# First experts of a decoder kernel: the residual add in four tiles, and a root of nine operations

## The reference

```
x = x + attention0(ln(x));  x = x + cross0(ln(x), ctx)
x = x + experts0(ln(x));    x = x + states(ln(x))
x = x + cross1(ln(x), ctx); x = x + experts1(ln(x))

ln(v)    = (v - mean) / sqrt(var + 1e-5)
experts0 = sum over 8 experts e of c[:, e] * ((silu(v W1 + B1) * (v W3 + B3)) W2 + B2)
           + a shared expert of the same form with weight 1
```

## Time and profile before

| | |
|---|---|
| median of 3 runs | 332.16 us |
| the profiled execution | 332.09 us |
| its span, first to last instruction | 330.4 us |
| mean granted TensorE clock | 0.906 |
| TensorE busy (matmul) | 267.2 us, 81% |
| VectorE busy | 216.7 us, 66% |
| ScalarE busy | 147.4 us, 45% |
| GpSimd busy | 63.6 us, 19% |
| chain that ended last | TensorE 40%, VectorE 13%, ScalarE 3% of the span |

### The profile page before, as it was taken

The page is one execution under the profiler, slowest core; times in us unless marked ns, Lnnn a source line. Parts: engine busy times, 40 slices in busy tenths (PEclk is TensorE's granted clock), DMA queues, the critical chain, the costliest instruction groups (busy, mean ns, idle before and its releaser), DMA issues.

```text
span 330.4 us, 5158 instructions
## 1 busy us (share of the span) xinstructions
PE 267.2 (81%) x1783; PEld 178.8 (54%) x1788; DVE 216.7 (66%) x775; ACT 147.4 (45%) x298; POOL 63.6 (19%) x71
## 2 busy tenths in 40 slices
PE   0898799995885889599499438863898989999994
PEld 0344677775542456456266224352387855666774
DVE  4638695697348546516823887799057768888974
ACT  2174654552440496344545402512445665444442
POOL 4346880000000034211423300112213000000000
PEclk9999799998796999879979756985699999999999
DMA  6368900029210000000000000000000000000002
GB/s 165 65 199 200 285 15 0 2 32 285 36 32 0 2 0 1 3 1 0 0 0 2 0 1 0 0 2 2 0 3 2 3 2 1 0 2 0 3 0 64
DMA packets 22038, 11.62 MB, mean 35 GB/s; under 512 B 11016, under 2 KB 21005, under 8 KB 22013
## 3 DMA queue, kind: packets, MB, share of 16 engines
q1 hardware_dynamic: 21117, 11.01, 13.0%
q0 software_dynamic: 80, 0.20, 0.6%
q10 hardware_dynamic: 816, 0.10, 0.2%
HBM read 8.68 MB, written 2.62 MB: 34 GB/s over the span
## 4 chain that ended last, share of the span: by engine, by line
PE 40%; DVE 13%; ACT 3%; issue 2%; DVEq 0%; ACTq 0%
PE bank L874 8%; PE bank L862 7%; PE bank L792 3%; PE bank L755 3%; PE bank L732 3%; PE bank L738 2%; PE bank L847 2%; PE bank L811 2%; DVE XN L1372 2%; PE bank L526 1%; DVE stats L1330 1%; PE bank L774 1%; PE bank L834 1%; DVE Es L1600 1%; DVE sm L1597 1%
## 5 line engine op out<-in xcount | busy, mean ns | idle before, releaser
L498 POOL TENSOR_TENSOR X<-X,att 128x512 f32<-128x512 f32 x18 | 22.8, 1269 | 116.2 <-ACT att L1182 116.2
L1546 DVE SCALAR_TENSOR_TENSOR att<-bank,cols,att 128x512 f32<-128x512 f32 x18 | 13.5, 751 | 27.1 <-ACT att L1171 14.6
L874 PE MATMUL bank<-Wb,att 128*128 128x128 f32 x256 | 30.8, 277 | 0.0
L874 PEld LDWEIGHTS bank<-Wb,att 128*128 128x128 f32 x256 | 29.7, 192 | 1.4 <-issue 1.4
L862 PE MATMUL bank<-XT,Wb 128*128 128x512 f32 x64 | 30.0, 599 | 0.0
L526 PE MATMUL bank<-ident,XN 128*128 128x128 f32 x48 | 10.0, 344 | 24.0 <-DVE XN L1372 24.0
L1182 ACT ACTIVATE att<-bank,comb 128x128 f32<-128x128 f32 x72 | 20.5, 370 | 18.2 <-PE bank L755 11.6
L755 PEld LDWEIGHTS bank<-W2a,att 128*128 128x128 f32 x144 | 20.3, 204 | 10.4 <-issue 5.2
L755 PE MATMUL bank<-W2a,att 128*128 128x128 f32 x144 | 22.3, 295 | 2.1 <-DVE att L1546 2.1
L1218 ACT ACTIVATE att<-bank 128x512 f32<-128x512 f32 x32 | 18.8, 598 | 9.1 <-PE bank L862 9.1
L526 PEld LDWEIGHTS bank<-ident,XN 128*128 128x128 f32 x48 | 6.9, 176 | 28.6 <-DVE XN L1372 25.8
(11 more groups left out here) (235 smaller groups left out, 544.7 us busy)
## 6 DMA issues: line engine op xcount, KB each, us to landing
Wb<-in_L_ffn_W SPq DMA_DIRECT2D x1, 1024.0 KB, 5.6
Wb<-in_L_ffn_W SPq DMA_DIRECT2D x8, 128.0 KB, 5.3
X<-in_x SPq DMA_DIRECT2D x2, 256.0 KB, 3.0
k_scratch<-QKVT SPq DMA_DIRECT2D x1, 512.0 KB, 2.6
q_scratch<-QKVT SPq DMA_DIRECT2D x1, 512.0 KB, 3.1
Wb<-k_scratch SPq DMA_DIRECT2D x1, 512.0 KB, 4.8
V<-q_scratch SPq DMA_DIRECT2D x1, 512.0 KB, 5.5
v_scratch<-QKVT SPq DMA_DIRECT2D x1, 512.0 KB, 6.1
```

Of the source, the lines that this page charges most:

```text
L498: nc.gpsimd.tensor_tensor(X[:, h * HT:(h + 1) * HT, :], X[:, h * HT:(h + 1) * HT, :], part0[:, i % 2, :, :], ALU.add).then_inc(f_acc, 1)
L874: last = mm(bank[4 + h][:, t * P:(t + 1) * P], hid[:, e % 2, f, tile], W2b[:, e, f, :], start=(f == 0), stop=(f == F1 - 1))
```

## The change

GpSimd adds tile by tile: four operations of 128 x 128 for each step, each of which waits for its own tile of `part0` and for the same tile's add of the step before. So ScalarE raises `f_part` after each tile, and the other waits for the two semaphores count tiles. The root's guess becomes one operation (the bits of var, read as an integer, times -0.5 plus the constant, written as an integer), and both steps are replaced by one polynomial of fourth degree in y = r*r*var: nine operations in the same three pieces, four, three and two. The tile `magic` and its semaphore go.

```diff
+    ROOT = (2.46301634, -3.28812578, 2.96127482, -1.41023935, 0.27407397)
...
-            nc.gpsimd.memset(magic[:, :], 0x5f3759df).then_inc(c_magic, 1)
...
-                    pool.wait_ge(f_part, i + 1)
-                    if i >= 1:
-                        pool.wait_ge(f_acc, i)
-                    nc.gpsimd.tensor_tensor(X[:, h * HT:(h + 1) * HT, :], X[:, h * HT:(h + 1) * HT, :],
-                                            part0[:, i % 2, :, :], ALU.add).then_inc(f_acc, 1)
+                    for t in range(HT):
+                        pool.wait_ge(f_part, HT * i + t + 1)
+                        if i >= 1:
+                            pool.wait_ge(f_acc, HT * (i - 1) + t + 1)
+                        nc.gpsimd.tensor_tensor(X[:, h * HT + t, :], X[:, h * HT + t, :], part0[:, i % 2, t, :],
+                                                ALU.add).then_inc(f_acc, 1)
...
-                    pe.wait_ge(f_part, i - 1)
+                    pe.wait_ge(f_part, HT * (i - 1))
...
-                    pe.wait_ge(f_part, 2 * (E0 + 1))
+                    pe.wait_ge(f_part, 2 * HT * (E0 + 1))
...
-                    act.wait_ge(f_acc, i - 1)
+                    act.wait_ge(f_acc, HT * (i - 1))
                 for t in range(HT):
                     tt = HT * h + t
-                    last = AF(part0[:, i % 2, t, :], bank[4 + i % 2][:, t * P:(t + 1) * P], ACT.Copy,
-                              scale=comb[:, tt, e:e + 1])
-                last.then_inc(f_part, 1)
+                    AF(part0[:, i % 2, t, :], bank[4 + i % 2][:, t * P:(t + 1) * P], ACT.Copy,
+                       scale=comb[:, tt, e:e + 1]).then_inc(f_part, 1)
...
             def root_guess(h):
-                r, var, bits = rs[:, 0, tiles(h)], rs[:, 1, tiles(h)], rs[:, 4, tiles(h)]
+                r, var, y, t = (rs[:, i, tiles(h)] for i in range(4))
                 then(V.tensor_scalar(var, mv[:, tiles(h), 1], EPS, None, ALU.add))
-                then(V.tensor_scalar(bits.bitcast(int32), var.bitcast(int32), 1, None, ALU.logical_shift_right))
-                then(V.tensor_tensor(r.bitcast(int32), magic[:, :], bits.bitcast(int32), ALU.subtract))
+                then(V.tensor_scalar(r.bitcast(int32), var.bitcast(int32), -0.5, float(0x5f3759df), ALU.mult, ALU.add))
+                then(V.tensor_tensor(t, r, r, ALU.mult))
+                then(V.tensor_tensor(y, t, var, ALU.mult))
 
             def root_third(h):
-                r, var, y2, p = (rs[:, i, tiles(h)] for i in range(4))
-                then(V.tensor_tensor(y2, r, r, ALU.mult))
-                then(V.tensor_tensor(y2, y2, var, ALU.mult))
-                then(V.tensor_scalar(p, y2, 0.375, -1.25, ALU.mult, ALU.add))
-                then(V.tensor_tensor(p, p, y2, ALU.mult))
-                then(V.scalar_tensor_tensor(r, p, 1.875, r, ALU.add, ALU.mult))
+                y, t = rs[:, 2, tiles(h)], rs[:, 3, tiles(h)]
+                then(V.tensor_scalar(t, y, ROOT[4], ROOT[3], ALU.mult, ALU.add))
+                then(V.tensor_tensor(t, t, y, ALU.mult))
+                then(V.scalar_tensor_tensor(t, t, ROOT[2], y, ALU.add, ALU.mult))
 
             def root_second(h):
-                r, var, y2, p = (rs[:, i, tiles(h)] for i in range(4))
-                then(V.tensor_tensor(y2, r, r, ALU.mult))
-                then(V.scalar_tensor_tensor(p, y2, -0.5, var, ALU.mult, ALU.mult))
-                then(V.scalar_tensor_tensor(r, p, 1.5, r, ALU.add, ALU.mult))
+                r, y, t = rs[:, 0, tiles(h)], rs[:, 2, tiles(h)], rs[:, 3, tiles(h)]
+                then(V.scalar_tensor_tensor(t, t, ROOT[1], y, ALU.add, ALU.mult))
+                then(V.scalar_tensor_tensor(r, t, ROOT[0], r, ALU.add, ALU.mult))
...
-                    dve.wait_ge(f_acc, (E0 + 1) * (h + 1))
+                    dve.wait_ge(f_acc, HT * (E0 + 1) * (h + 1))
```

More of the change, by code:

```diff
@@ L90, in decoder_kernel @@
         jconst = sb("jconst", [P, NC, E1], int32)
-        magic = sb("magic", [P, HT], int32)
         vecs = sb("vecs", [31, P])
@@ L209, in decoder_kernel @@
         c_ident = sem("c_ident")
-        c_magic = sem("c_magic")
         c_azero = sem("c_azero")
@@ L1398, in first_max @@
                 then(V.tensor_tensor(one_hot, em8[:, cut, :], per_row(rv[:, 4, cut], E0), ALU.is_equal))
-            dve.wait_ge(c_magic, 1)
             for h in range(2):
```

## The result

| | before | after |
|---|---|---|
| median of four runs each, same chip, us | 332.75 (332.11 to 333.63) | 320.80 (320.44 to 321.50) |
| ratio to before | 1 | 0.965 (0.962 to 0.968) |
| profiled execution, us | 332.09 | 321.50 |
| its span, us | 330.4 | 319.8 |
| its mean granted clock | 0.906 | 0.915 |

The change takes 12 us away, 3.5%. Forecast were 327.9 us and a range of 325.4 to 330.2: the sign was right and the size far too small. The profiled executions differ by 10.6 us, and these 10.6 us are what the traces can account for. Executions in the slower of the chip's two states are left out of every comparison; the only one is the first profiled execution of the kernel before kept busy (330.7 us, the other three 325.2 to 326.1).

A forecast was written before the change was run, and what follows sets the result against it. Neither TensorE nor VectorE alone was the bound: work changes hands where TensorE waits for VectorE's XN. From 332.09 us, 3.8 for roots and 0.4 for holds came off, giving 327.9 us, range 325.4 to 330.2.

The forecast's parts named there:

- The roots, 3.8 us: Layer norms' roots on VectorE: nine operations for eleven save 0.40 us each where TensorE waits; 3.8 us, bounds 2.2 to 4.2.
- The holds, 0.4 us booked: VectorE's root operations held by GpSimd's adds: 4.4 us instead of 5.1, 0.7 gained on paper, 0.4 booked.
- rival (c): TensorE's lower clock after idling, at 137 to 146 us or behind 165 and 194: 325.5 or 330.3; chance faster 0.12, slower 0.05.
- (a): GpSimd/VectorE port: VectorE can't get between tile adds, stalls grow by 1.8 us, 330.1 us; chance 0.15.
- (b): Roots of the run's first half are hidden: they save 2.2 us instead of 3.8, 329.5 us; chance 0.07.
- (d): ScalarE's writes, 116 to 186 us: signalling each breaks their overlap, 0.34 us a group, 334.0 us; chance 0.03.
- (e): GpSimd's add still waits for all four tiles, 328.3 us; chance 0.58 together with the forecast.
- The test named in advance: Mean granted clock off 0.906 by more than 0.01 would show that (c), not the roots, made the difference.

The follow-up runs named there:

- kernel before kept busy: Kernel before plus 10 and 12 unread bf16 matmuls (the fillers) ahead of the transposes at 137.01 and 164.99: 325.69 us, ratio 0.983; again 325.51 us, 0.982.
- The root alone: Kernel after with one add of 128x512 and one signal a group again, keeping the new nine-operation root: 327.17 us, ratio 0.988 to the kernel before.
- the second execution: Kernel after run once more, unchanged, with a second profile: 320.61 us, ratio 0.964 to the kernel before, span 318.7.
- the pauses: Kernel after with seven more 4-element products (1.4 us) behind the root at each of two places: 326.68 us, ratio 0.986 to the kernel before.
- the late version: Kernel after, but each of the four adds waits until all four tiles are written: 323.77 us, ratio 0.974 to the kernel before.

## Why the prediction was wrong in size

**The roots, 3.8 us: right.** The root alone gave 4.0 us, but 1.6 of its profiled gain were clock, so that this number agrees partly by luck; the waits show the term better. At undisturbed places XN is ready 0.39 us sooner, with nine operations 0.2 apart, and the int32 guess lasts 0.17 like its neighbours. One of the nine was lost in the profiled execution: the first transposes start 0.32 us sooner (8.18 for 8.50), and the first scores 0.2 later (29.46 for 29.27), with the next transposes taking 0.99 us in the kernel after for 0.60 in the one before. That is not the clock, which was granted 1.00 there in both, and in the second execution they take 0.60 and the scores start at 28.43. The waits that the roots shorten sum to some 3.5 us.

**The holds, 0.4 us booked: the first step that failed.** They fell from 5.1 to 2.5 us, a gain of 2.6. The prediction gave a held operation 0.36 us and let it delay the adds. In the trace a held operation lasts 0.38, so it waits 0.21, and the adds don't wait for VectorE: four take 1.69 whether it is between them or not. The start-to-start distance is (1.69 - 0.456)/3 = 0.41 us, so the 0.40 was right; what was wrong is the cycle around it. The next add has already begun while the released operation runs its 0.17, so from one release to the next it is 0.41 us in all, of which 0.17 are the operation and 0.03 lie between two of them; 0.21 are left as the hold. Against the change the Trainium skill (GPSIMD Engine Reference, Elementwise — side-by-side cycle accounting) had led to an estimate of 0.44 for a tile; measured are 0.456 for one alone and 0.41 in a row. It changed little: by the working above the hold hangs on the pace and not on the length.

**The gate's hold: left out.** The prediction does not mention it, and so put it at nothing without a reason. In the kernel before, an operation inside the gate of the second half was held. Timeline of VectorE, then of TensorE:

```profile
151.74 1.13 DVE L1395 TENSOR_TENSOR rt<-rt,rv 128x32 f32<-128x32 f32 x1
```

```profile
158.70 1.16 PE L755 MATMUL bank<-W2a,att 128*128 128x128 f32 x8 [0.83 <-DVE att L1546]
```

Against the ordinary 0.19 us it was held 0.94; in the kernel after two of the gate's operations last 0.41 and 0.34, held 0.37 together. ScalarE waits for the gate's result before it weighs an expert's output (4.00 us of idling, ended at 156.08 by L1537; 3.43 in the kernel after). Its silu, VectorE's product and TensorE's matmul follow in turn, and the wait at the last of them falls from 0.83 us to 0.26 (at 152.76). These 0.57 us belong to the same term: the holds gave 3.1 us in all where 0.4 stood.

**The clock, rival (c), 12%: the second step that failed.** It stood beside the forecast as an accident, at "about 2.4 us" for half of a stretch; half of the 3.4 us that it had worked out is 1.7, so the 2.4 has no working. TensorE's timeline gives its real size: from XN's transpose at 137.01 to the expert matmuls at 145.29 the kernel before loses 3.3 us to the kernel after (5.37 of shift less 2.04 already there), and behind 166 us another 1.6: 4.9 us on the path, both stretches whole. The fillers give the same 3.3 and 1.6 us with VectorE's work untouched, the pauses take them away again. The prediction had named the two places and the idling, and its 3.4 us for the first was nearly right; but it did not let the shorter waits of its own sum carry the clock with them. Roots and holds together took 1.3 and 1.1 us off these two waits, and behind both the level was low.

**Sum over the profiled executions.** Roots gave 3.5 and holds with the gate's 3.1; of the 10.6 us that leaves 4.0 for the clock and everything else. The two stretches gave 4.9, and 0.9 were lost elsewhere, some 0.4 ahead of 137 us and the rest behind 194 us. One such loss lies from 83 to 88 us, 1.2 us: the matmuls at L543 took 1.92 us for 1.51 and those at L546 1.91 for 1.02, at the low level. The second execution of the kernel after divides otherwise: of its 11.7 us the two stretches hold 3.3, and 1.8 come from elsewhere. So where the clock pays differs from execution to execution. Both leave 4 to 5 us beyond roots and holds, of which 4.9 and 3.3 are shown to be the clock's at the two places.

**The rivals.** (a), the port turned against the change: refuted, nothing is held longer than one tile's add. (b): only one of the four early roots was lost. (d): refuted, four writes with four signals take 1.14 us as with one. (e): the adds do begin when written; the late version costs 3 us. The test named in advance, a mean clock off 0.906 by more than 0.01, sounded in the second profile (0.923) and not quite in the first (0.915), because the mean mixes the two stretches gained with the ones that grew at 77 and 101 us.

**What stays open.** Why the first stretch is granted 1.00 in one execution and 0.86 in another at the same idling of 1.49 us: what decides the level besides this one wait is not shown. The kernel before itself lies anywhere from 330.2 to 333.8 us in its runs, and the kernel after from 320.3 to 321.5; how the 12 us of the medians divide is known only as far as the profiled executions go.

## What to carry to other kernels

When a change shortens a wait of TensorE, look at the granted clock behind that wait before you sum: if it is low there, add what the same matmuls cost at the two levels (here 2.06 us against 1.10 for one pair, 1.6 and 3.3 us for whole stretches) as a part of the forecast, not as a rival, and ask whether unread matmuls would give the same for less. Where small operations of VectorE run beside GpSimd's tensor adds, small adds hold them less (2.5 us for four pieces, 3.4 for two, 5.1 for one), and an early start puts more of the adds under work that isn't held, such as the moments. Two edits that cut the same wait are to be costed together.

## What the runs showed that was not expected

- A GpSimd add of two fp32 tensors lasts 0.200 us for 128x4, 0.456 for 128x128, 0.725 for 128x256, 1.269 for 128x512. From 128x128 up a further 128 columns cost 0.27 us; back to back, 128x128 adds start 0.41 us apart.
- With small adds the two engines take turns one by one: one held operation of VectorE per add, 0.21 us each, and the adds keep their pace (four in 1.69 to 1.73 us) as if VectorE were not there.
- Two stretches of idling of 2.8 and 3.4 us cost the kernel before 4.9 us of its 332 in lower clock behind them, more than the root edit's own 3.5; 22 short matmuls that nobody reads recovered them.
- An execution's granted clock isn't the same from run to run in a given stretch (1.00 and 0.86 in the first of the two), though the kernel after stays within 1.2 us in eight executions.
